# Linear attention of the first block: packed 16-row products replaced by full-array products on 128-token chunks

## The reference, cut to what matters

```python
# conditioning: r = x, k = v = side input
decay = exp(-exp(w)) * (0.5 + 0.5 * tf)        # tf = sigmoid(sum(time_emb))
ek = exp(minimum(k, 30)); ekv = ek * v
nf, df = scan over tokens of (a * decay + ekv, b * decay + ek)     # and nb, db in reverse
euk = exp(minimum(u + k, 30))
num, den = nf + nb - ekv + euk * v, df + db - ek + euk
out = sigmoid(r) * (num / maximum(den, 1e-8)) * (0.8 + 0.2 * tf)

# linear attention, 16 heads of 16 channels, 2 chunks of 128 tokens
h = rmsnorm(x, qkv_norm_w, 2**-23)
q, k, v = split(h @ ternary(qkv_w).T)          # ternary: round(w / mean|w|) in {-1, 0, 1} * mean|w|
mask[t, s] = exp(-s_h * (t - s)) if t >= s else 0
scores = q @ k.T * mask
o = 0.25 * (scores @ v + (q * lam_t) @ S)      # S: 16 x 16 state of the chunk before
S = lam_T * S + (k * lam_rev).T @ v
out = rmsnorm(rmsnorm(o, norm_w, 1e-6), proj_norm_w, 2**-23) @ ternary(proj_w).T
x = x + out
```

## Time and profile before

| | us |
|---|---|
| median of 3 runs | 2029.68 (2028.22 to 2039.93) |
| profiled execution, own time | 2035.18 |
| its span, first to last instruction | 2033.9 |
| start and projections, up to the first score (0 to 118.6) | 118.6 |
| attention pairs (118.6 to 209.9) | 91.3 |
| two norms, projection, residual (209.9 to 253.5) | 43.6 |
| the seven stages behind | 1780.4 |

### The profile page before, as it was taken

How to read it: one execution, slowest core, us unless ns; L and a number is a source line. 1 busy time by engine, 2 the same in 40 slices (tenths; PEclk the granted TensorE clock), 3 DMA queues, 4 the chain that set the end, 5 groups by cost and what they waited for, 6 DMA issues and landing times.

```text
span 2033.9 us, 16567 instructions
## 1 busy us (share of the span) xinstructions
PE 1648.3 (81%) x5375; PEld 885.9 (44%) x5386; DVE 1279.3 (63%) x2046; ACT 913.6 (45%) x1581; POOL 357.1 (18%) x233
## 2 busy tenths in 40 slices
PE   0599788878877999986798989876667777689998
PEld 0255354436753434433344444432312332247776
DVE  7476346634433653546778787748768799955665
ACT  4311525433332211225878787734555453324444
POOL 5000032223100010000000000000025665502332
PEclk9975789988676999998899999876778899989999
DMA  2000076426003000001101010100100000021110
GB/s 86 0 1 1 0 261 217 155 64 104 1 1 126 0 0 0 0 1 55 47 1 44 1 44 1 39 33 17 44 0 0 1 0 0 0 68 44 53 47 27
DMA packets 40043, 80.68 MB, mean 40 GB/s; under 512 B 8882, under 2 KB 26116, under 8 KB 37398
## 3 DMA queue, kind: packets, MB, share of 16 engines
q1 hardware_dynamic: 34870, 53.93, 8.7%
q0 software_dynamic: 5088, 25.69, 3.6%
HBM read 71.34 MB, written 7.22 MB: 39 GB/s over the span
## 4 chain that ended last, share of the span: by engine, by line
PE 29%; DVE 12%; ACT 7%; issue 4%; POOL 2%; DMA 0%; PEldq 0%; POOLq 0%; DVEq 0%; SPq 0%; ACTq 0%; PEld 0%
PE bank L157 21%; PE bank L2510 3%; PE bank L1895 2%; POOL s_bu L2426 2%; DVE s_bu L2322 1%; DVE s_bu L2314 1%; DVE g_q L1593 1%; DVE g_turn L1591 1%; DVE g_turn L1592 1%; PE bank L2446 1%; PE bank L1885 1%; PE bank L1876 1%; DVE g_q L1597 1%; DVE g_rs L1584 1%; DVE q_g L2070 1%
## 5 line engine op out<-in xcount | busy, mean ns | idle before, releaser
L2426 POOL TENSOR_TENSOR s_bu<-s_rep,s_du 128x1024 f32<-128x1024 f32 x64 | 151.5, 2371 | 718.0 <-DVE s_du L2306 607.7
L2314 DVE TENSOR_TENSOR_SCAN s_bu<-bank,s_bu 128x1024 f32<-128x1024 f32 x64 | 146.0, 2282 | 21.1 <-ACT bank L2388 10.1
L2510 PE MATMUL bank<-s_bu,ident 128*128 128x512 f32 x256 | 132.8, 645 | 1.0 <-DVE s_dl L2263 0.3
L2388 ACT ACTIVATE bank<-s_dl,s_an 128x510 f32<-128x510 f32 x128 | 83.0, 682 | 106.3 <-DVE s_bu L2314 106.2
L157 PE MATMUL bank<-e_xs,e_wsp 128*128 128x512 f32 x528 | 127.8, 391 | 0.7 <-issue 0.7
L157 PEld LDWEIGHTS bank<-e_xs,e_wsp 128*128 128x128 f32 x528 | 99.0, 188 | 22.8 <-issue 1.9
L157 PE MATMUL bank<-r_am,r_b 128*128 128x512 f32 x240 | 108.8, 593 | 0.0
L157 PE MATMUL bank<-conditioned,g_wqk 128*128 128x512 f32 x160 | 88.2, 680 | 7.4 <-DVE g_wqk L1578 7.4
L2446 PE MATMUL bank<-s_bc,s_pick 96*128 96x512 bf16 x128 | 42.0, 412 | 56.9 <-DVE s_bu L2322 55.5
L1420 POOL TENSOR_TENSOR r_ys<-r_y,r_y 128x512 f32<-128x512 f32 x14 | 22.8, 1631 | 342.0 <-DVE r_y L1365 342.0
L2322 DVE TENSOR_TENSOR s_bu<-s_bu,bank 128x1024 f32<-128x1024 f32 x64 | 76.7, 1199 | 4.3 <-PE bank L2446 4.2
(11 more groups left out here) (452 smaller groups left out, 3783.6 us busy)
## 6 DMA issues: line engine op xcount, KB each, us to landing
e_wgu<-in_e_gu SPq DMA_DIRECT2D x22, 256.0 KB, 2.7
b_vw<-b_values SPq DMA_DIRECT2D x48, 64.0 KB, 3.4
e_wd<-in_e_down SPq DMA_DIRECT2D x22, 128.0 KB, 2.6
r_w<-in_r_w SPq DMA_DIRECT2D x3, 896.0 KB, 8.2
g_wqk<-in_g_qk SPq DMA_DIRECT2D x4, 640.0 KB, 4.1
g_wgv<-in_g_gv SPq DMA_DIRECT2D x4, 640.0 KB, 4.4
g_wo<-in_g_wo SPq DMA_DIRECT2D x4, 512.0 KB, 3.6
m_sorted<-m_zero SPq DMA_DIRECT2D x1, 1920.0 KB, 12.8
```

The lines of the kernel that those rows point to most:

```text
L2314: e.tensor_tensor_scan(b, flat(k.pairs[n % 2][:, :, :]), b, 0.0, ALU.mult, ALU.add).then_inc(k["s_scanned"].up(), 1)
L2388: e.activation(banks[2 * (n % 2) + i][:, :].rearrange("p (b t) -> p b t", t=T)[:, :, 1:T], m.dl[:, et, half(h)].rearrange("p (b t) -> p b ...
L2426: e.tensor_tensor(m.bu[n % m.NBU][:, :, :], m.rep[:, 2 * np:2 * np + 2, :], m.du[:, et, half(h)].unsqueeze(1).to_broadcast([P, 2, HALF]), ...
L2510: summed = e.matmul(banks[6][:, :], k.ident[:, :], m.bu[(n - 1) % m.NBU][:, i, :], start=np == 0 and i == 0, stop=np == m.NP - 1 and i == ...
```

## The change

Only the first stage is rewritten. These parts are changed together:

- The side input is loaded in two halves of 512 tokens, the first factor is made half by half and tile by tile (quarters 0 to 3), and the three additions of numerator and of denominator become accumulating products with the identity on PE (`first_den_tensor`, `first_num_tensor`). The sigmoid of the time gate is made of an exponential and a reciprocal.
- The attention of the first half of the tokens starts as soon as its own quarters are there; the second norm half, projections of queries and keys, and values are made inside the attention's loop.
- Heads are not padded: a tile holds 8 heads of 16 channels. The queries of a tile are spread into 8 copies, each with all rows but those of one head set to zero (6 on ScalarE, 2 on VectorE), so that keys (128 rows) times one copy gives one head's scores. Values lie in blocks of 144 columns of which 16 are filled, so that 8 products of 128 x 128 accumulate all heads of a unit in one bank.
- A unit is one chunk of 128 tokens and one tile of 8 heads: 16 units instead of 32 pairs. Masks are 128 x 128. What the second chunk sees of the first goes through a state of 128 x 128, cut to its diagonal blocks.
- The two norms at the end become one (weights squared into the matrix of ones, a constant of 2^-23 added to it, the product of both norm weights applied once), and its first half and projection lie inside the loop.

The diff, cut to its core:

```diff
@@ start, SP and DVE
-    e.dma_start(k.kv[:, :, :], d["side"]).then_inc(k["load_side"].up(16), 16)
+    e.dma_start(k.kv[:, :, half(0)], d["side"][:, :, half(0)]).then_inc(k["load_side0"].up(16), 16)
+    e.dma_start(k.kv[:, :, half(1)], d["side"][:, :, half(1)]).then_inc(k["load_side1"].up(16), 16)
-    run_out(wkv_vector(k, e, [(0, 0), (0, 1)]))
+    first_back(k, e, 0)
+    start_capped(k, e, 1)
+    first_back(k, e, 1)
+    start_weighted(k, e, 0)
+    first_terms(k, e, 0)
+    first_cap(k, e, 0)
+    first_cap(k, e, 1)
+    first_terms(k, e, 1)
+    start_gain(k, e, 1)
+    first_factor(k, e, 0)
+    start_weighted(k, e, 1)
+    first_factor(k, e, 1)
+    first_condition(k, e, 0)
@@ the sums on PE
+def first_den_tensor(k, e, q):
+    ct = q % 2
+    e.wait_ge(*k["first_back"].at(4 * q + 4))
+    e.wait_ge(*k["first_euk"].at(q + 1))
+    if q >= 2:
+        e.wait_ge(*k["first_capped"].at(q - 1))
+    mm(e, k.banks[2 + ct][:, :], [(k.ident[:, :], a[:, half(ct)]) for a in (k.df, k.nb[1], k.euk)]).then_inc(k["first_den"].up(), 1)
@@ linear_vector, before the loop
+    ternary_mean(k, e, m.wqkv, m.partq, "load_l0_qkv")
+    ternary_round(k, e, m.wqkv, m.partq, 768 * C, 0, banks[7][:, 0:1])
+    first_back(k, e, 2)
+    norm_apply(k, e, 0, 0, k.XC, m.rs, "l0_qkv_norm", m.sq)
+    first_back(k, e, 3)
+    first_cap(k, e, 2)
+    linear_spread_vector(k, e, 0)
+    first_cap(k, e, 3)
+    first_terms(k, e, 2)
+    first_terms(k, e, 3)
+    first_factor(k, e, 2)
...
+    first_factor(k, e, 3)
+    first_condition(k, e, 1)
@@ the spread on ACT
+    for j in range(m.BY_VECTOR, 8):
+        e.activation(m.bdq[i][:, j, :], m.qs[i][:, :], ACT.Copy, scale=m.heads[:, j:j + 1]).then_inc(k["l0_spread"].up(), 1)
@@ linear_tensor, the loop
+    e.wait_ge(*k["first_ready"].at(4))
+    for n in range(m.UNITS + 1):
...
+            for g in range(2):
+                last = e.matmul(k.pairs[1 + n % 2][:, g, :], m.kb[i][:, tile(u)], m.bdq[i][:, tile(g, 4), tile(u)], start=True, stop=True, skip_group_check=True)
...
+        if n + 1 < m.UNITS:
+            linear_values_tensor(k, e, n + 1)
...
+        if u == 2 and p < 3:
+            linear_query_tensor(k, e, p + 1)
+        if u == 3 and p < 3:
+            linear_key_tensor(k, e, p + 1)
...
+            for j in range(8):
+                last = e.matmul(dst, v[:, tile(j)], sm[:, j, :], start=j == 0, stop=j == 7 and o % 2 == 0, skip_group_check=True)
+            if o % 2:
+                e.wait_ge(*k["l0_state_out"].at(o // 2 + 1))
+                last = e.matmul(dst, m.st[o // 2 % 2][:, :], m.ql[o // 4 % 2][:, o % 4 // 2, :], start=False, stop=True, skip_group_check=True)
@@ linear_vector, the loop
+            e.tensor_tensor(flat(m.sm[n % 3][:, :, :]), flat(k.pairs[1 + n % 2][:, :, :]), flat(m.decm[:, tile(p % 2, 8), :]),
+                            ALU.mult).then_inc(k["l0_masked"].up(), 1)
...
+        if n >= 4:
+            step(background, 4)
@@ linear_scalar, behind the loop
-    norm_scalar(k, e, 1, m.q4, m.k4, m.rs, 1e-6, (k["l0_out"], 0), 8)
-    norm_scalar(k, e, 2, m.q4, m.k4, m.rs, 2.0 ** -23, (k["normed"], 2), 1)
+    e.activation(m.qs[0][:, :], banks[6][:, :], ACT.Square, scale=0.25).then_inc(k["l0_squares"].up(), 1)
+    e.mul(m.o[:, 1, half(1)], banks[6][:, :], 0.25).then_inc(k["l0_out"].up(), 1)
+    norm_root(k, e, 1, 1, m.rs, 2.0 ** -23 * 1e-6, banks[2])
```

More of the change, by code:

```diff
@@ L281, in norm_scalar, with norm_apply @@
+def norm_apply(k, e, n, h, src, rs, wname, dst):
+    e.wait_ge(*k["inverse_root"].at(2 * n + h + 1))
+    for ct in range(CT):
+        last = e.scalar_tensor_tensor(dst[:, ct, half(h)], src[:, ct, half(h)], k.vcol(wname, ct), rs[:, half(h)], ALU.mult, ALU.mult)
+    last.then_inc(k["normed"].up(), 1)
+def norm_scalar(k, e, n, src, sq, rs, eps, first):
+    signal, ready = first
     for h in range(NH):
-        e.wait_ge(*signal.at(before + each * (h + 1)))
-        e.activation(sq[:, :, half(h)], src[:, :, half(h)], ACT.Square).then_inc(k["squares"].up(), 1)
+        norm_square(k, e, src, sq, h, (signal, ready + h + 1))
@@ L364, in start_scalar @@
     e.activation(wv, wv, ACT.Exp, scale=-1.0).then_inc(k["decay_exp"].up(), 1)
[L365 to L367 removed]
+    e.wait_ge(*k["time_sum"].at(1))
+    e.activation(k.tf[:, :], k.tf[:, :], ACT.Exp, scale=-1.0).then_inc(k["time_exp"].up(), 1)
+    start_exp(k, e, 0)
+    first_exp(k, e, 0)
+    first_exp(k, e, 1)
+    start_exp(k, e, 1)
+    linear_decays(k, e)
@@ new lines, in start_scalar @@
+    e.wait_ge(*k["load_x"].at(16))
+    for h in range(NH):
+        e.activation(k.XC[:, :, half(h)], k.XT[:, :, half(h)], ACT.Sigmoid).then_inc(k["sigmoid"].up(), 1)
+    first_inverse(k, e, 0)
+def first_den_tensor(k, e, q):
+    ct = q % 2
+    e.wait_ge(*k["first_back"].at(4 * q + 4))
+    e.wait_ge(*k["first_euk"].at(q + 1))
+    if q >= 2:
+        e.wait_ge(*k["first_capped"].at(q - 1))
+    mm(e, k.banks[2 + ct][:, :], [(k.ident[:, :], a[:, half(ct)]) for a in (k.df, k.nb[1], k.euk)]).then_inc(k["first_den"].up(), 1)
@@ new lines, in linear_tensor @@
+    e.wait_ge(*k["l0_masked"].at(m.UNITS))
+    for c, a in enumerate((m.kb[0], m.qs[0])):
+        e.wait_ge(*k["l0_squares"].at(c + 1))
+        last = e.matmul(banks[2][:, :], m.wsq[:, c, :], a[:, :], start=c == 0, stop=c == CT - 1, skip_group_check=True)
+    last.then_inc(k["square_sums"].up(), 1)
+    e.wait_ge(*k["normed"].at(4))
+    for ct in range(CT):
+        mm(e, banks[3 + ct][:, :], [(m.wp[:, c, tile(ct)], m.o[:, c, half(1)]) for c in range(CT)]).then_inc(k["l0_projected"].up(), 1)
```

582 lines of the change are left out of this document (376 added, 206 removed).

## The result

The changed kernel took 1948.7 us (median of four executions, 1943.0 to 1951.4), the kernel before 2029.0 beside it: a ratio of 0.958 with a 95% interval of 0.955 to 0.961. The forecast was 1943 with a range of 1926 to 1980. The profiled execution took 1951.4 us with a span of 1950.2; of the kernel before it was 2035.2 and 2033.9.

The account below looks back on a forecast made before the run. The prediction took a DVE-led chain to bound the start, PE at half clock the attention, and ACT, PE and DVE in turn the end. -58.6 - 1.3 - 26.6 = -86.5 us, from the 2029.7 median, gave 1943; range 1926 to 1980.

Parts of the forecast that it names:

- Part 1: Start up to the loop's first score: a chain led by DVE falls from 118.6 to 60 us, 58.6 less.
- the additions taken off DVE: In the start, eight additions of 1.23 us, 9.8 us of DVE, go to PE as 24 matmuls.
- Part 2: Attention loop: 91.3 becomes 90 us, from 85 us of PE work, 3 of stalls and 2 of slow start.
- the 3 us for stalls in units 8 and 9: In the loop, factor additions and second rounding meet there, costing DVE 6 us each against PE's 4.5.
- The 2 us for a start at 1.2 GHz: Allowance of 2 us in the loop for PE beginning at half clock.
- The clock was the choice that mattered: Loop: nearly all products 128 x 128 x 128 or wider would be granted full clock, against 0.52 for the old packed loop.
- 2.85 us of packed work at full clock, half of 5.7, against 4.3: Loop, per unit: packed 5.7 us at 1.2 GHz, 2.85 at 2.4; new form 4.3 at full clock, 8.6 at half.
- Part 3, 43.6 becomes 17: Behind the last mixing: ACT's inverse 4.6 us late, then square, root, product, projections and addition; 26.6 us less.
- the 1780.4 us behind are untouched: Later stages behind the three rewritten windows: taken to keep their 1780.4 us.
- Rival (a): Hand-overs between neighbouring units bound the loop: 6.5 us a unit instead of 5.3, 20 us more, 1963; chance 0.17.
- (b): The full array does not get full clock: loop 170 instead of 90 us, 2023, no change; chance 0.05.
- (c): Loop at half clock with weight loads of 128-column products uncovered: 78 us more, 2101, slower; chance 0.02.

Follow-up runs that it names:

- dve_sums: Changed kernel with the first factor's additions back on DVE and the 24 identity products on PE left away: 1950.4 us, ratio 0.958, stage end 167.9 against 163.2 us.
- whole: Changed kernel with the first half's conditioning, norm, projections and spreading moved behind the whole first factor, every instruction kept: 1967.7 us, ratio 0.967.
- rows32: Changed kernel with the attention's score and mixing products contracting 32 rows instead of 128: 1985.7 us, ratio 0.976; loop granted clock 0.71.
- before_fill40: Kernel before with four added, unread products of 40 rows ahead of each pair's scores: 2097 us, ratio 1.031.
- before_fill: Kernel before with four added, unread products of 128 x 128 x 128 ahead of each pair's scores: 2028.5 us against 2033.1, ratio 0.997.
- two_norms: Changed kernel with the second half's two scalings made one after the other again: 1952.3 us, ratio 0.958; stage end 170.7 us, 7.5 later.
- The two paces: Changed kernel with five next-factor steps per unit for four: 1945.0 us; with 6, 6, 4, 0, 0 in the last five units and added PE products: 1946.3 us.

## Why the prediction was right

**Part 1, 118.6 becomes 60: it was 58.2.** The steps, forecast and measured: first cap at 7.8 and 6.65; first half multiplied in by 31 and 29.9; weights rounded by 37 and 35.7; scans and norm's product by 43.4 and 42.3; the third denominator's sums begun at 40 and 39.25, and done in 4.4 us for 4.7 (the first of the three at 1.2 GHz, the last at full clock); last factor by 59.4 and 58.15. About 1 us of the lead is the first cap's, and it stays constant down the chain. Two prices were off without moving the sum: the first twelve sums of PE were priced at 1.2 GHz and ran at full clock from the third on, but they lay beside DVE's scans either way; and the additions taken off DVE were put at 9.8 us, where dve_sums shows 4.6 for having the sums on PE. One slip helped by luck: behind the sums at 49 the listed steps of DVE (0.7, 6.2, 0.6, 1.3 and 0.7) add up to 58.5, not 59.4, and the 0.9 us too many stand where DVE really waited 0.45 and 0.88 us, for which the list has nothing. That the halves are what takes the projections out of the chain is shown: 16.8 us of the gain (whole).

**Part 2, 91.3 becomes 90: it was 88.7.** PE's sum was 85 and 85.70. Of the 3 us for stalls in units 8 and 9 one of 1.68 came, in unit 9, and one of 1.03 in unit 0. The 2 us for a start at 1.2 GHz were not spent, because the second half's sums had run until 57.4; in dve_sums, without them, the start was at 1.2 GHz. DVE had 66.75 us of work, not 71.

**The clock was the choice that mattered, and it was right for the reason given.** rows32 and before_fill40 take rows away at equal instructions and lose it, before_fill adds filled products to the old loop and gets it. That is shown for rows; the 32 columns, which the prediction names beside them, stay untested. The rule of the Trainium skill, "TensorE: Matmul & The Clock Gate" (Part 3, Packing small matmuls), that short contractions belong in row groups side by side, holds in these traces at equal clock: 3.26 us a unit packed against 3.5 for the same scores and mixing. It does not tell what decided here, that the packed loop was granted 0.52. The forecast had weighed 2.85 us of packed work at full clock, half of 5.7, against 4.3. Packed it was 3.26, and the 4.3 hold the unit's values, which the old kernel makes ahead of its loop; without them it was 3.8. Packing is worth less here than the forecast said.

**Part 3, 43.6 becomes 17: it was 16.4.** ACT's inverse ended 2.5 us behind the last mixing, not 4.6, and the last projections took 6.7 us instead of 5.2 because PE was at 1.2 GHz for all but the last of them. The shape was right and two terms were off against each other. The merged norm is 7.5 us of the gain in the second half's chain (two_norms); the rest is what moved into the loop.

**The sum.** Forecast were -86.5 us for the stage, measured -90.2. The total missed in the other direction, 1948.7 for 1943: between the medians lie 80.3 us. Of the 9.9 us between that and 90.2, 6.5 are the later stages of this pair of profiles, and the rest comes from the profiled executions, which stood 6.2 us above the median before and 2.7 above it after. The step that failed is the one that took no working: "the 1780.4 us behind are untouched". Their code is, their time is not. They scatter over 14 us in steps, so one profiled pair can't place a total more closely than that, whatever the stage does. The prediction should have widened its own range by it and might have seen it in the times: the three executions of the kernel before that were shown spread over 12 us.

Rival (a), hand-overs as the bound, fails on the second window: waits of PE add up to 3 us. The two paces showed that it lies near: a pause of 2.2 to 2.4 us in one unit cost the pause and some 1.7 us more in clock. Rivals (b) and (c) fail on the clock of 1.00.

## What to carry to other kernels

Where a busy PE is granted half its clock, ask over how many rows its products run before asking how many products there are; an unpacked form, slower at equal clock, can be the faster one, and a few filled products whose result nobody reads can test that. A pause of PE can be paid twice, in the wait and in the products behind it: those of 2.2, 2.4, 4.3, 4.8 and 5.8 us above were, one of 2.57 us (at 290.68 in the kernel before) was not. Where the row behind a pause is slow, fill the pause or move what causes it; and a step that waits for another engine must not stand ahead of one that PE waits for. Measure a change of one stage by that stage's end in the profile: here 4.7 and 7.5 us were plain there and invisible in the total.

## What the runs showed of the hardware

Added work made a kernel faster: 256 matrix instructions more, 8.6 us less in the stage and 4.7 in the median. With half of them the same program fell into either of two times, 2015 to 2027 or 2063 to 2075 us, from one execution to the next. A product over 32 rows took as long at full clock as one over 128 (1.88 us for four instructions of 512 columns), and a loop that is mostly such products was granted 0.71. And the fetch of the same tokens, issued at the same place, kept PE waiting for 3.7 to 6.7 us in thirteen profiles and not at all in one.
